# Feed-forward stages of layers 2 and 3: FP4 rounding step from a ScalarE square, work of neighbouring units interleaved

## The reference, cut to what matters

```
def fp4_quant_dequant(x):
    xb = x.reshape(shape[:-1] + (shape[-1] // BLOCK, BLOCK))
    scale = jnp.max(jnp.abs(xb), axis=-1, keepdims=True) / 6.0
    scale = jnp.maximum(scale, jnp.float32(1e-12))
    xn = xb / scale
    idx = jnp.searchsorted(_MID, jnp.abs(xn))
    q = _GRID[idx] * jnp.sign(xn) * scale      # grid 0 .5 1 1.5 2 3 4 6
...
gate = fp4_linear(x, w_gate)                   # 128 -> 352
y = fp4_linear(x, w_up)
h = jax.nn.silu(gate) * y
return fp4_linear(h, w_down)                   # 352 -> 128
```

## Time and profile before

| | |
|---|---|
| time, median of 3 runs | 4230.71 us (4229.49 to 4238.97) |
| span of the profiled execution | 4250.5 us |
| busy: TensorE, VectorE, ScalarE, GpSimd | 68%, 65%, 40%, 48% of the span |
| mean granted TensorE clock | 0.817 of full speed |
| the four feed-forward stages, first `x_v` to last `hq` | 675.1 us together |

### The profile page before, as it was taken

One profiled execution on the slowest core, in us unless ns is written; L12 is line 12 of the kernel. 1 busy time (PEld: TensorE's weight loads), 2 busy tenths in 40 slices (PEclk: granted clock), 3 DMA queues, 4 the chain that ended last, 5 costly groups with the idle time before them and its releaser, 6 DMA issues. The chain is left out here.

```text
span 4250.5 us, 64084 instructions
## 1 busy us (share of the span) xinstructions
PE 2877.9 (68%) x22097; PEld 1782.5 (42%) x22097; DVE 2748.4 (65%) x5884; ACT 1703.2 (40%) x2994; POOL 2032.5 (48%) x2683
## 2 busy tenths in 40 slices
PE   5848367775493659659488746687565888467846
PEld 3748312221493338449233334233243333244534
DVE  4634468884344852343588669688497887595678
ACT  2413147675131314334265612466422566224511
POOL 6643332210433222232365467355595564585686
PEclk9869669997597759869699868799786999686967
DMA  5113132210121012002212000222001221000000
GB/s 166 42 54 90 38 104 81 81 56 27 57 87 50 0 50 72 19 19 67 75 70 84 32 1 0 89 72 84 2 1 46 76 77 47 0 1 1 1 0 20
DMA packets 217155, 206.14 MB, mean 48 GB/s; under 512 B 49432, under 2 KB 194008, under 8 KB 216073
## 3 DMA queue, kind: packets, MB, share of 16 engines
q1 hardware_dynamic: 204552, 176.85, 12.9%
q0 software_dynamic: 12288, 25.19, 1.9%
HBM read 103.55 MB, written 96.47 MB: 47 GB/s over the span
## 5 line engine op out<-in xcount | busy, mean ns | idle before, releaser
L979 DVE TENSOR_REDUCE l0b_negm<-l0b_ps_s 128x2 f32<-128x1024 f32 x256 | 304.2, 1220 | 50.7 <-PE l0b_ps_s L732 49.7
L822 ACT ACTIVATE l0b_E<-l0b_ps_t 128x1024 f32<-128x1024 f32 x256 | 262.0, 1023 | 132.4 <-PE l0b_ps_t L714 132.2
L822 ACT ACTIVATE l2a_E<-l2a_ps_t 128x768 f32<-128x768 f32 (+1 forms) x192 | 169.4, 882 | 134.0 <-PE l2a_ps_t L714 133.2
L822 ACT ACTIVATE l3a_E<-l3a_ps_t 128x768 f32<-128x768 f32 (+1 forms) x192 | 169.4, 882 | 127.6 <-PE l3a_ps_t L714 126.7
L979 DVE TENSOR_REDUCE l2b_negm<-l2b_ps_s 128x2 f32<-128x256 f32 (+3 forms) x256 | 196.4, 818 | 27.5 <-PE l2b_ps_s L737 27.3
L822 ACT ACTIVATE l2b_E<-l2b_ps_t 128x768 f32<-128x768 f32 (+1 forms) x192 | 169.3, 882 | 106.6 <-PE l2b_ps_t L714 105.8
L979 DVE TENSOR_REDUCE l3a_negm<-l3a_ps_s 128x2 f32<-128x256 f32 (+3 forms) x256 | 196.3, 819 | 17.1 <-PE l3a_ps_s L737 17.0
L979 DVE TENSOR_REDUCE l2a_negm<-l2a_ps_s 128x2 f32<-128x256 f32 (+3 forms) x256 | 196.0, 818 | 17.3 <-PE l2a_ps_s L737 17.2
L899 POOL TENSOR_SCALAR_AFFINE_SELECT l2b_E<-l2b_E 128x256 f32<-128x256 f32 x256 | 100.7, 409 | 177.3 <-ACT l2b_E L822 177.3
L899 POOL TENSOR_SCALAR_AFFINE_SELECT l2a_E<-l2a_E 128x256 f32<-128x256 f32 x256 | 101.5, 409 | 170.8 <-ACT l2a_E L822 169.0
L899 POOL TENSOR_SCALAR_AFFINE_SELECT l3a_E<-l3a_E 128x256 f32<-128x256 f32 x256 | 101.6, 409 | 163.4 <-ACT l3a_E L822 161.5
...
## 6 DMA issues: line engine op xcount, KB each, us to landing
...
```

The source lines that it names most:

```text
L822: act.activation(probs(n % 3, c, 0)[:, 2 * p:2 * p + 2, :], ps_t[:, :, 0:width[c]], ACT.Exp, scale=scale).then_inc(probs_ready.sem, 1)
L979: e = dve.tensor_reduce(negm[:, qt, :, j], ps_s[n % 2][:, :, off:off + keys[qt]], AX.X, ALU.max, negate=True)
```

## The change

In `quantized_ffn_stage` only:

- The number that rounds is now made from the square of the divided value: base plus a constant times v squared. ScalarE makes the square. For h it makes only the square (`squares`, one 128x704 operation), and VectorE adds the base inside its add and its subtract (`scalar_tensor_tensor` in `round_h`), so the two operations that made `power` are gone. For x it makes square and sum (`steps_x`, two 128x256 operations), and GpSimd keeps four of its nine operations.
- Quantising is cut in two, `divide_h` and `round_h`, `divide_x` and `round_x`, with other units' work between; `v`, `scale`, `square`, `x_v` and `x_step` have two buffers.
- TensorE takes x three units ahead instead of one, and puts the input products in front of the output products; ScalarE's list follows.
- One more GpSimd memset (128x1, `grid_base`) in the load stage.

```diff
+GRID_BASE = 1.2 * 2.0 ** 22
+GRID_SCALE = math.sqrt(0.8 * 2.0 ** 22) / 2.12
...
+            def divide_x(u):
+                pool.wait_ge(x_inv_ready.sem, x_inv_ready.upto(u // 2 + 1))
+                if u >= 2:
+                    pool.wait_ge(xq_ready.sem, xq_ready.upto(u - 1))
+                pool.tensor_tensor(x_v[u % 2][:, :, :], blocks(x_tiles(u)), wide(x_inv[u // 2 % 2][:, half(u)], NX),
+                                   ALU.mult).then_inc(x_v_ready.sem, 1)
+
+            def round_x(u):
+                pool.wait_ge(x_step_ready.sem, x_step_ready.upto(u + 1))
...
-                ch.link(pool.tensor_tensor(x_square[:, :, :], x_v[:, :, :], x_v[:, :, :], ALU.mult))
-                pool.tensor_scalar(x_power[:, :, :], x_square[:, :, :], 4.0, MAGIC, ALU.is_ge, ALU.mult)
-                ch.link(pool.tensor_scalar(x_square[:, :, :], x_square[:, :, :], 16.0, 2.0 * MAGIC, ALU.is_ge, ALU.mult))
-                ch.link(pool.tensor_tensor(x_power[:, :, :], x_power[:, :, :], x_square[:, :, :], ALU.add))
-                ch.link(pool.tensor_scalar(x_power[:, :, :], x_power[:, :, :], MAGIC, None, ALU.add))
...
+            divide_x(0)
             for u in range(ALL):
-                quantize_x(u)
+                if u + 1 < ALL:
+                    divide_x(u + 1)
+                round_x(u)
...
+            def round_h(u):
+                dve.wait_ge(squares_ready.sem, squares_ready.upto(u + 1))
...
+                ch.link(dve.scalar_tensor_tensor(x, q, GRID_BASE, x, ALU.add, ALU.add))
+                ch.link(dve.scalar_tensor_tensor(x, q, GRID_BASE, x, ALU.add, ALU.subtract, reverse1=True))
+                dve.tensor_tensor(blocks(hq[u % 2][:, :, :]), x, wide(scale[u % 2][:, :], NH), ALU.mult).then_inc(quant_ready.sem, 1)
...
+            multiply(0)
+            divide_h(0)
             for u in range(ALL):
-                for t in range(T2):
-                    multiply(u, t)
-                if u % 2 == 1 and u // 2 + 2 < B:
+                if u + 1 < ALL:
+                    multiply(u + 1)
+                    divide_h(u + 1)
+                if u % 2 == 0 and u // 2 + 2 < B:
                     scales_x(u // 2 + 2)
-                quantize_h(u)
+                round_h(u)
                 if u >= 1:
                     add(u - 1)
...
             for u in range(ALL):
-                if u + 1 < ALL:
-                    input_products(u + 1)
-                if u + 2 < ALL:
-                    transpose_x(u + 2)
                 transpose_h(u)
+                if u + 3 < ALL:
+                    input_products(u + 3)
                 output_products(u)
+                if u + 4 < ALL:
+                    transpose_x(u + 4)
...
+                act.activation(x_step[u % 2][:, :, :], x_v[u % 2][:, :, :], ACT.Square, scale=GRID_SCALE).then_inc(x_squared, 1)
+                act.wait_ge(x_squared, u + 1)
+                act.activation(x_step[u % 2][:, :, :], x_step[u % 2][:, :, :], ACT.Identity, bias=core.grid_base[:, :]).then_inc(x_step_ready.sem, 1)
...
             for u in range(ALL):
-                if u + 1 < ALL:
-                    gates(u + 1)
-                if u + 2 < ALL:
-                    read_xT(u + 2)
-                read_hT(u)
+                if u + 3 < ALL:
+                    read_xT(u + 3)
+                read_hT(u)
+                if u + 4 < ALL:
+                    steps_x(u + 4)
+                if u + 2 < ALL:
+                    squares(u + 2)
+                if u + 3 < ALL:
+                    gates(u + 3)
```

More of the change, by code:

```diff
@@ L148 @@
     "row_mean_ready",
+    "x_v_ready",
+    "x_step_ready",
     "row_stats_ready",
@@ L277, in _ @@
             pool.memset(core.onesb[:, :], 1.0).then_inc(made, 1)
+            pool.memset(core.grid_base[:, :], GRID_BASE).then_inc(made, 1)
             pool.memset(core.earlier[:, :], 1.0).then_inc(made, 1)
@@ L3128, in quantized_ffn_stage @@
         x_inv = [sb(f"x_inv{u}", [P, 2 * NX]) for u in range(2)]
-        x_v = sb("x_v", [P, NX, BLOCK])
-        x_square = sb("x_square", [P, NX, BLOCK])
-        x_power = sb("x_power", [P, NX, BLOCK])
+        x_v = [sb(f"x_v{u}", [P, NX, BLOCK]) for u in range(2)]
+        x_step = [sb(f"x_step{u}", [P, NX, BLOCK]) for u in range(2)]
         xq = [sb(f"xq{u}", [P, T2, D]) for u in range(2)]
@@ L3135, in quantized_ffn_stage @@
         h = sb("h", [P, T2, HID])
-        scale = sb("scale", [P, NH])
+        scale = [sb(f"scale{u}", [P, NH]) for u in range(2)]
         inv = sb("inv", [P, NH])
-        v = sb("v", [P, NH, BLOCK])
-        power = sb("power", [P, NH, BLOCK])
+        v = [sb(f"v{u}", [P, NH, BLOCK]) for u in range(2)]
+        square = [sb(f"square{u}", [P, NH, BLOCK]) for u in range(2)]
         hq = [sb(f"hq{u}", [P, T2, HID]) for u in range(2)]
@@ L3159, in x_tiles, with half @@
             return core.XN[:, u * T2:(u + 1) * T2, :]
+        def half(u):
+            return slice(u % 2 * NX, (u % 2 + 1) * NX)
         @block.gpsimd
@@ L3174, in quantize_x @@
-                pool.tensor_scalar(x_power[:, :, :], x_square[:, :, :], 4.0, MAGIC, ALU.is_ge, ALU.mult)
-                ch.link(pool.tensor_scalar(x_square[:, :, :], x_square[:, :, :], 16.0, 2.0 * MAGIC, ALU.is_ge, ALU.mult))
-                ch.link(pool.tensor_tensor(x_power[:, :, :], x_power[:, :, :], x_square[:, :, :], ALU.add))
-                ch.link(pool.tensor_scalar(x_power[:, :, :], x_power[:, :, :], MAGIC, None, ALU.add))
-                ch.link(pool.tensor_tensor(x_v[:, :, :], x_v[:, :, :], x_power[:, :, :], ALU.add))
@@ L3179, in quantize_x @@
-                ch.link(pool.tensor_tensor(x_v[:, :, :], x_v[:, :, :], x_power[:, :, :], ALU.subtract))
-                pool.tensor_tensor(blocks(xq[u % 2][:, :, :]), x_v[:, :, :], wide(x_scale[u // 2 % 2][:, half], NX),
+                x, p = x_v[u % 2][:, :, :], x_step[u % 2][:, :, :]
+                ch.link(pool.tensor_tensor(x, x, p, ALU.add))
+                ch.link(pool.tensor_tensor(x, x, p, ALU.subtract))
+                pool.tensor_tensor(blocks(xq[u % 2][:, :, :]), x, wide(x_scale[u // 2 % 2][:, half(u)], NX),
```

67 lines of the change are left out of this document (41 added, 26 removed).

## The result

The changed kernel takes 4142.25 us (median of 4 runs, 4136.59 to 4146.13), the kernel before in the same session 4233.33. The ratio is 0.9783, 95% interval 0.9767 to 0.9799: 2.2% faster. The forecast was 4155, its range 4112 to 4190.

What follows compares the result with a forecast made beforehand. VectorE was taken to bound, GpSimd close behind. A stage summed to 14.2 + 6 x 18.5 + 22.0 + 2.7 = 149.9 us against 168.8, 75.6 less in four stages: 4230.7 - 75.6 = 4155 us, range 4112 to 4190.

Steps and rivals of the forecast that it cites:

- first `x_v` to iteration 0: Start of a stage: first `h` at 8.3 us, a new 1.3 us wait for unit 1's gates, iteration 0 at 14.2.
- what follows the last `hq`: End of a stage, after its last `hq`: claimed to be unchanged, so put at nothing in the sum.
- The pair: Two units in VectorE's loop, one batch of x scales: even iteration 9.4 plus odd 9.1, 18.5 us instead of 20.06.
- Clean unit: One unit on VectorE with GpSimd already done: 7.88 less 1.12 for two `power` operations, 6.76 us.
- Contention: VectorE slowed where it meets GpSimd operations, 0.4 us each: 1.2 in an even iteration, 1.0 in an odd one.
- Stall: VectorE's `add` in the odd iteration waits 1.3 us for output products that TensorE finishes late.
- at its lower level from about 1.8 us after the gap on: TensorE's clock after idling for `xq`: input products done at 5.7 us, output products take 2.93, done at 8.7.
- Rival 1: TensorE stays at the upper clock level, no wait: pair 17.1, stage 140.5, 4118 us; chance 0.22.
- Rivals 2 and 3: 2: TensorE at lower clock throughout, 4187 us, chance 0.16; 3: GpSimd operations delay VectorE by their clean length, 4199, 0.06.
- Rival 4: VectorE's scalar_tensor_tensor takes two passes at 128x704, 0.89 us more each: pair 20.7, 4235 us, no change; chance 0.06.
- rival 5: Slower: x transposes waiting for a late `xq` hold TensorE; at 4 us late, pair 22.5, 4243 us; chance 0.06.
- the way to be wrong: ScalarE's list holds `gates` so long that `multiply` waits in the steady loop; costed at nothing.

Runs made afterwards that it cites:

- gap_filled: The changed kernel with 14 transposes that nobody reads added on TensorE after the output products of each odd unit; 4127.02 us, ratio 0.9741.
- scales_early: The changed kernel with a third batch of x scales in the prologue and each later batch one iteration earlier; 4120.07 us, ratio 0.9721.
- gates_ahead_of_squares: The changed kernel with ScalarE's gates of unit u+3 put ahead of the square of unit u+2; 4128.44 us, ratio 0.9754.

## Why the prediction was right, and where it was off

The sign and most of the mechanism held: VectorE's `power` operations and most of its contention went, scalar_tensor_tensor costs what tensor_tensor does (883 and 891 ns where nothing stretches it, against 891), and ScalarE's new operations cost nothing in the loop. The changed kernel's tile views of `v` and `x_v` answer to the earlier trace rows:

```profile
L3323 ACT ACTIVATE l3fb_square<-l3fb_v x16: 772/790/792, 3990.7 to 4112.9; 128x704 f32<-128x704 f32 x16
L3234 DVE SCALAR_TENSOR_TENSOR l3fb_v<-l3fb_square,l3fb_v x16: 883/884/1418, 3996.9 to 4115.8; 128x704 f32<-128x704 f32 x16
L3235 DVE SCALAR_TENSOR_TENSOR l3fb_v<-l3fb_square,l3fb_v x16: 891/1192/1407, 3997.9 to 4116.7; 128x704 f32<-128x704 f32 x16
L3189 POOL TENSOR_TENSOR l3fb_x_v<-l3fb_x_v,l3fb_x_step x16: 724/731/1367, 3978.7 to 4097.2; 128x256 f32<-128x256 f32 x16
```

The sum of one stage, term by term, in `l3fb`:

| term | predicted | measured |
|---|---|---|
| first `x_v` to iteration 0 | 14.2 | 14.9 |
| six pairs | 6 x 18.5 = 111.0 | 103.1 |
| three iterations | 22.0 | 20.8 |
| last rounding | 2.7 | 2.7 |
| stage | 149.9 | 141.5 |
| what follows the last `hq` | unchanged | 1.5 longer |

- **The pair, 1.4 us too long.** Clean unit: 6.60, not 6.76 (0.32 a pair), mostly since the first rounding operation no longer waits for the one before it (0.81 us from start to start instead of 0.93). Contention: 0.3 + 0.4 in the even and 0.5 + 0.4 in the odd iteration, 1.6 instead of 2.2. Stall: 0.8 instead of 1.3. So 2 x 6.60 + 1.42 + 1.6 + 0.8 = 17.0, and 17.12 measured.
- **The stall's step that failed** was "at its lower level from about 1.8 us after the gap on". The level was low at the end of the gap already and had risen before the output products, which took 1.50 and not 2.93. That the wait exists, once per pair in front of `add`, and goes when the clock stays up, is shown by the pairs within gap_filled; that the gap comes from the late scales, and that the wait goes with it though the clock still falls, by scales_early.
- **Rival 1's pair, 17.1, and its stage, 140.5 (141.0 measured), are the measured ones, but not for its reason**: it had the upper level throughout and no wait. At that level a pair takes 8.71 + 7.43 = 16.1 (gap_filled).
- **"What follows the last `hq` is unchanged"** was wrong by 1.5 us a stage, 6 in all. From the end of the last `hq` to the start of the last `add` it was 5.1 us (4235.69 to 4240.77) and is 6.6 (4118.53 to 4125.08), because unit 14's output products now stand in front of the last `hq` transposes. Before and after:

```profile
4240.77 0.42 DVE L3217 TENSOR_TENSOR X<-X,l3fb_ps_o 128x256 f32<-128x256 f32 x1 [4.75 <-PE l3fb_ps_o L3269]
```

```profile
4125.08 0.42 DVE L3241 TENSOR_TENSOR X<-X,l3fb_ps_o 128x256 f32<-128x256 f32 x1 [4.31 <-PE l3fb_ps_o L3296]
```

- **The start**: the first `h` comes 8.4 us after the first `x_v` (8.3 predicted), with the new wait for the second unit's gates at 1.21 (1.3).
- **Rivals 2 and 3** had TensorE without pauses and rounding operations of 1.5 us and more; neither is there; the longest rounding operation is 1.42. Rival 3 was the rule of the Trainium skill, page "Perfetto Trace Analysis", section "Optimizing Scalar/DVE Operations", on the port that VectorE and GpSimd share, read strictly. The runs disagree with this reading: of four GpSimd operations of 0.73 a pair, VectorE gets back 0.8 us, not 2.9. **Rival 4** (two passes) fell with 884 ns, **rival 5** with `xq` done 1.0 us into the odd iteration (0.35 predicted). What I called the way to be wrong, ScalarE's list holding `gates` in the steady loop, does not occur. Its mirror image, gates that hold a square, I had not priced; it needs the old order, and there it costs 204 us.
- **GpSimd** is busy 61.7 us of a stage and not 75: fewer of its operations are stretched than I had counted (in `l3fb` 10 of 16 divisions took 0.62 us and 9 of 16 additions 0.72 or 0.73).
- **A slip in rival 5**: a pair of 22.5 us gives 4155 + 24 x 4 = 4251 by the forecast's own sum, not 4243.

The stages give 4 x 27.8 = 111 us, 35 more than predicted; the tails take 6 back. The medians differ by 91, which leaves 14. In the traces, from the first `x_v` of `l2fa` to the end, 94.2 us go, so 11 us are lost between the stages. From the last `add` of one feed-forward stage to the first `x_v` of the next, three of them added, it was 1060.2 us before and 1071.0 in the changed kernel, but 1063.2 to 1071.4 in the twelve experiments, which all share that code; gates_ahead_of_squares has the longest. I can't tie it to the change; its cause stays open. The first 2484 us of the profiled execution of the kernel before, again the same code, were 21.4 us longer than those of the changed kernel: the 19.8 us between its span and its median were no constant to be carried over.

So that 4155 lies only 13 us from the measured time is partly luck: the stages were 35 us too long in the sum, and a longer tail and longer stretches between the stages, both put at nothing, gave back about half of it.
